# The bias of an output projection, moved from a TensorE product and a ScalarE copy to one VectorE pass, in a four-engine attention pipeline

## The reference

```python
h = jnp.maximum(_layernorm(x, axis=-1), 0.0)
x = x + _L0_gnn_ref(h, adj, adj, L0_gnn_b)          # (128, 128, 256) + a number per row
h = jnp.maximum(_layernorm(x, axis=-1), 0.0)
...
qkv = (x @ w_qkv).reshape(b, n, 3, H, hd).transpose(2, 0, 3, 1, 4)      # 8 heads of 32
attn = jnp.einsum('bhnd,bhmd->bhnm', q, k) * scale
attn = jnp.where(attn_mask[None, None] == 0, -jnp.inf, attn)
attn = jax.nn.softmax(attn, axis=-1)
o = jnp.einsum('bhnm,bhmd->bhnd', attn, v).transpose(0, 2, 1, 3).reshape(b, n, d)
o = o @ w_proj + b_proj
mu = jnp.mean(o, axis=-1, keepdims=True)
var = jnp.mean(jnp.square(o - mu), axis=-1, keepdims=True)
ln = (o - mu) * jax.lax.rsqrt(var + LN_EPS) * ln_gamma + ln_beta
return o + ln
```

## Time and profile before

| | us |
|---|---|
| median of 3 runs | 870.18 |
| lowest, highest | 869.18, 874.16 |
| profiled execution, its own time | 871.38 |
| its span | 869.7 |
| PE busy | 765.6 (88%) |
| DVE busy | 613.9 (71%) |
| ACT busy | 500.7 (58%) |
| POOL busy | 424.7 (49%) |

### The profile page before, as it was taken

How to read it: one execution, slowest core, us unless ns; L and a number is a source line. 1 busy time by engine, 2 the same in 40 slices (tenths; PEclk the granted TensorE clock), 3 DMA queues, 4 the chain that set the end, 5 groups by cost and what they waited for, 6 DMA issues and landing times.

```text
span 869.7 us, 31246 instructions
## 1 busy us (share of the span) xinstructions
PE 765.6 (88%) x11241; PEld 518.0 (60%) x11241; DVE 613.9 (71%) x1552; ACT 500.7 (58%) x1192; POOL 424.7 (49%) x853
## 2 busy tenths in 40 slices
...
GB/s 190 64 155 145 124 159 138 173 145 128 168 163 137 155 151 159 104 171 163 141 159 169 128 137 160 156 150 172 157 137 146 162 148 166 129 133 120 51 46 25
DMA packets 167271, 121.34 MB, mean 140 GB/s; under 512 B 83696, under 2 KB 166384, under 8 KB 166640
## 3 DMA queue, kind: packets, MB, share of 16 engines
...
q0 software_dynamic: 16896, 16.78, 14.2%
...
## 4 chain that ended last, share of the span: by engine, by line
PE 72%; issue 8%; ACT 6%; DVE 5%; SPq 3%; POOL 3%; DMA 2%; ACTq 1%; DVEq 0%; POOLq 0%
PE a_ps L319 17%; PE a_ps L332 9%; PE sum_ps L446 9%; PE pv_ps L416 8%; PE sc_ps L368 7%; PE sum_ps L419 6%; PE sc_ps L396 5%; PE sc_ps L344 4%; PE a_ps L304 4%; SPq L273 3%; DVE smax L674 2%; ACT h_sb L516 2%; PE pv_ps L431 2%; PE sum_ps L443 2%; ACT o_sb L590 1%
## 5 line engine op out<-in xcount | busy, mean ns | idle before, releaser
L674 DVE TENSOR_REDUCE smax<-sc_ps 128x4 f32<-128x512 f32 x256 | 164.8, 685 | 53.7 <-PE sc_ps L368 51.6
L571 ACT ACTIVATE p_sb<-sc_ps 128x512 f32<-128x512 f32 x256 | 145.8, 599 | 45.9 <-PE sum_ps L419 36.9
L666 DVE TENSOR_TENSOR pairs<-a_ps,pairs 128x512 f16<-128x512 f32 x128 | 87.5, 684 | 110.7 <-ACT pairs L561 110.2
L841 POOL TENSOR_TENSOR h_parts<-h_sb,h_parts 128x256 f16<-128x256 f32 x128 | 84.2, 669 | 141.5 <-ACT h_parts L524 141.2
L319 PE MATMUL a_ps<-hT,w_hi 128*128 128x512 f16 x512 | 141.0, 400 | 13.7 <-DMA hT<-h_parts 13.7
L847 POOL TENSOR_TENSOR oT_lo<-oT,oT_hi 128x256 f16<-128x256 f32 x128 | 85.6, 669 | 119.5 <-ACT oT_hi L584 119.3
L561 ACT ACTIVATE pairs<-a_ps 128x512 f16<-128x512 f32 x128 | 75.9, 594 | 97.8 <-PE a_ps L319 85.0
L416 PE MATMUL pv_ps<-p_sb,v_sb 128*32 128x128 f32 x2048 | 107.6, 279 | 20.1 <-DVE crow L680 10.3
L878 POOL DMA_DIRECT2D out<-y_sb x32 | 43.6, 1363 | 141.4 <-DVE y_sb L730 141.4
L419 PE MATMUL sum_ps<-p_sb,sel_sum 128*32 128x128 f32 x2048 | 105.3, 274 | 0.0
L368 PE MATMUL sc_ps<-stack 96*128 96x128 f16 x1024 | 86.0, 226 | 6.7 <-DMA stack<-pairs 6.5
...
## 6 DMA issues: line engine op xcount, KB each, us to landing
...
stack<-crow SPq DMA_DIRECT2D x64, 8.0 KB, 3.9
...
hT<-h_parts ACTq DMA_TRANSPOSE x32, 6.0
```

Source lines behind the costliest of these rows:

```text
L571: nc.scalar.activation(p_sb[:, u % P_SLOTS], sc_ps[u % SC_SLOTS][:], ACT.Exp, scale=SCALE).then_inc(p_ready, 1)
L666: nc.vector.tensor_tensor(pairs[:, 1 - c % 2, c // 2, c % 2], a_ps[c % 2][:], pairs[:, c % 2, c // 2, c % 2], ALU.subtract).then_inc(qklo_ ...
L674: nc.vector.tensor_reduce(smax[:, HC * j:HC * (j + 1), b], sc_ps[u % SC_SLOTS][:], AX.X, ALU.max).then_inc(smax_ready, 1)
L841: nc.gpsimd.tensor_tensor(h_parts[:, par, 1, b], h_sb[:, b], h_parts[:, par, 0, b], ALU.subtract).then_inc(hlo_ready, 1)
```

## The change

The bias is no longer a product. `project_o` has six products instead of seven, and `take_o` goes from ACT to DVE: one `scalar_tensor_tensor` reads `o_ps`, scales it and adds the bias, which all partitions hold (`bproj_sb`). The constants that split the bias go away. The orders of PE, ACT, DVE and POOL are changed.

```diff
-ACT_CONST = 5
-DVE_CONST = 14 + 2
+ACT_CONST = 4
+DVE_CONST = 7
...
-                nc.tensor.matmul(o_ps, bias_ones[:], bp_rows[:], start=True, stop=False)
                 for k, (o, w) in enumerate(((oT_hi, wp_hi), (oT_hi, wp_lo), (oT_lo, wp_hi))):
                     for j in range(DC):
-                        mm = nc.tensor.matmul(o_ps, o[:, b, j], w[:, j], start=False, stop=(k == 2 and j == DC - 1))
+                        mm = nc.tensor.matmul(o_ps, o[:, b, j], w[:, j], start=(k == 0 and j == 0), stop=(k == 2 and j == DC - 1))
                 mm.then_inc(o_psum, 1)
...
-            ORDER = ("K0 S0 S1 R0 S2 Q0 S3 R1 Q1 N0 E0 R2 O0 E1 E2 E3 L0 O1 R3 K1 S4 S5 O2 S6 S7 L1 O3 N1 M0 E4 E5 E6 "
-                     "P0 P1 Q2 P2 P3 Q3 P4 P5 E7 V0 P6 P7 V1").split()
+            ORDER = ("K0 S0 S1 R0 S2 S3 Q0 R1 Q1 R2 N0 E0 E1 E2 O0 L0 E3 R3 O1 K1 S4 S5 S6 L1 O2 S7 O3 N1 M0 E4 P0 P1 "
+                     "Q2 E5 P2 P3 Q3 E6 E7 P4 P5 V0 P6 P7 V1").split()
...
-                nc.scalar.activation(bp_parts[:, 0], bproj_sb[:], ACT.Copy).then_inc(act_const, 1)
...
-            def take_o(g, b):
-                act.wait_ge(o_psum, G * g + b + 1)
-                if b == 0:
-                    wait(act, tw_ready, G * g)
-                nc.scalar.activation(o_sb[:, b], o_ps, ACT.Copy, scale=1.0 / (OS * WS)).then_inc(o_ready, 1)
...
+            def take_o(g, b):
+
+                dve.wait_ge(o_psum, G * g + b + 1)
+                if b == 0:
+                    wait(dve, tw_ready, G * g)
+                nc.vector.scalar_tensor_tensor(o_sb[:, b], o_ps, 1.0 / (OS * WS), bproj_sb[:], ALU.mult,
+                                               ALU.add).then_inc(o_ready, 1)
...
-            ORDER = ("I0 I1 I2 S0 O0 S1 S2 S3 O1 Q0 O2 X0 Q1 L0 B0 O3 S4 B1 S5 S6 S7 B2 B3 M0 X1 G0 L1 Q2 F0 Q3 F1 F2 "
-                     "F3").split()
+            ORDER = ("I0 I1 I2 S0 O0 S1 S2 O1 S3 Q0 O2 X0 Q1 A0 O3 L0 A1 B0 S4 S5 B1 A2 S6 S7 A3 B2 M0 B3 G0 L1 F0 F1 "
+                     "Q2 F2 F3 Q3 X1").split()
...
-            ORDER = ("C0 Q0 R0 R1 C1 Q1 E0 C2 O0 E1 E2 E3 H0 O1 X0 C3 R2 O2 H1 H2 O3 R3 M0 H3 E4 A0 T0 Q2 A1 E5 Q3 E6 "
-                     "E7 A2 V0 A3 V1 L0").split()
...
+            ORDER = ("R0 C0 R1 H0 Q0 H1 Q1 C1 C2 E0 E1 E2 E3 X0 R2 H2 R3 C3 H3 M0 E4 A0 L0 T0 A1 Q2 E5 Q3 A2 E6 E7 A3 "
+                     "V0 V1").split()
```

More of the change, by code:

```diff
@@ L77, in build @@
         bproj_sb = sb("bproj_sb", [P, D])
-        bproj_r1 = sb("bproj_r1", [P, D])
-        bproj_r2 = sb("bproj_r2", [P, D])
         bias0_sb = sb("bias0_sb", [P, 1])
@@ L88, in build @@
         mask_k = sb("mask_k", [P, ROW_TILES, N], BF16)
-        bp_parts = sb("bp_parts", [P, 3, D], F16)
-        bp_rows = sb("bp_rows", [P, D], F16)
-        bias_ones = sb("bias_ones", [P, P], F16)
         identf = sb("identf", [P, P])
@@ L615, in step @@
                         take_pv(t - 2, i)
-                    elif kind == "O" and d:
-                        take_o(t - 3, i)
                     elif kind == "C" and d:
@@ L744, in step @@
                         scale_o(t - 3, i)
+                    elif kind == "A" and d:
+                        take_o(t - 3, i)
                     elif kind == "B" and d:
@@ L776, in later_constants @@
             def later_constants():
-                nc.vector.memset(bias_ones[:], OS * WS).then_inc(dve_const, 1)
-                nc.vector.memset(bp_rows[:], 0.0).then_inc(dve_const, 1)
                 nc.vector.tensor_scalar(mask_n[:, 0], adj_sb[:], 0.0, MASKED, ALU.is_equal, ALU.mult).then_inc(dve_const, 1)
@@ L788, in later_constants @@
                                         ALU.add).then_inc(dve_const, 1)
-                dve.wait_ge(act_const, 5)
-                nc.vector.tensor_tensor(bproj_r1[:], bproj_sb[:], bp_parts[:, 0], ALU.subtract).then_inc(dve_const, 1)
-                dve.wait_ge(dve_const, DVE_CONST - 6)
-                nc.vector.tensor_copy(bp_parts[:, 1], bproj_r1[:]).then_inc(dve_const, 1)
-                dve.wait_ge(dve_const, DVE_CONST - 5)
-                nc.vector.tensor_tensor(bproj_r2[:], bproj_r1[:], bp_parts[:, 1], ALU.subtract).then_inc(dve_const, 1)
-                dve.wait_ge(dve_const, DVE_CONST - 4)
-                nc.vector.tensor_copy(bp_parts[:, 2], bproj_r2[:]).then_inc(dve_const, 1)
-                dve.wait_ge(dve_const, DVE_CONST - 3)
-                for i in range(3):
-                    nc.vector.tensor_copy(bp_rows[HD * i:HD * i + 1], bp_parts[HD * i:HD * i + 1, i]).then_inc(dve_const, 1)
             stats_x(0, 0)
@@ L878, in store @@
                 nc.gpsimd.dma_start(og[g], y_sb[:], accum_op=ALU.add).then_inc(stored, 16)
-            ORDER = ("C0 C1 C2 H0 C3 H1 H2 H3 N0 W0 W1 W2 W3 K0 D0 X0").split()
+            ORDER = ("C0 C1 H0 C2 C3 H1 H2 H3 N0 W0 W1 K0 W2 W3 D0 X0").split()
             def step(t, k, a, sc, e, d, prep, norm, load):
```

## The result

The changed kernel took 908.49 us as a median of 4 runs (902.86 to 909.23), the kernel before 871.6 us as a median of 4 (869.18 to 874.16). The ratio is 1.0409, with a 95% interval of 1.0355 to 1.0463: 36.9 us slower, where 44 were forecast. The profiled execution took 908.0, its span is 906.2 us. Now and then a run is over 1.5% longer than the fastest of its kernel; the ratios leave such runs out (in o2_ahead two of four), the medians keep them.

What follows compares the result with a forecast made beforehand. PE was taken as the bound, with DVE tied at N1. Steps of +1.65 us (0.6 + 0.44 + 0.6) in 20, +0.95 in 9, and 2 at the start gave +44 us: 914, range 888 to 932.

Steps and rivals of the forecast that it cites:

- Term 1: DVE's queue ahead of N1: added takes make the eighth row maximum late, P0 +0.6 us per step.
- Term 2: PE behind P0: E5 and E6 now stand there, where PE is the bound, +0.44 us per step.
- the start: Before the full steps: Q0 and Q1 on ACT wait for POOL's shift, +2 us, bounds 0 and +3.
- the end: Last three steps: 0.1 less on PE and 0.04 more on the take per element cancel, 0.
- term 3: Second half of the stack: Q3 on DVE behind F delays its DMAs, S4 +0.6 us, between 0 and 1.2.
- the stalls: About 9 steps that begin with a stall: stack lateness counts nothing there, +0.95 us each, 9 us.
- The walk through the queues: Following PE's and DVE's new orders up to P0: eighth maximum ends at 12.3, N1 starts at 12.36.
- The rival of 948: New PE waits lower the clock in 20 steps, 1.7 us each; chance 0.10 shared with a slow take.

Runs made afterwards that it cites:

- o2_ahead: Changed kernel with O2 ahead of S6 on PE and B1 behind the last take on DVE; 894.02 us, ratio 1.0175 to the kernel before.
- stats_in_gap: Changed kernel with the statistics of x on DVE moved behind L1, where DVE waits for POOL; 908.76 us, ratio 1.0433 to the kernel before.
- e5_e6_ahead: Changed kernel with E5 and E6 ahead of P0 on PE, as before; 930.93 us, ratio 1.0634 to the kernel before.
- e5_e6_x_later: The e5_e6_ahead kernel with the load of x moved behind C3 on ACT; 906.73 us, ratio 1.0419 to the kernel before.
- all_undone: Changed kernel with O2, B1, E5, E6, Q2, Q3, X1, POOL's shift and the load of x moved, other orders kept; 878.04 us, ratio 1.0043.
- orders_alone: Kernel before, bias product on PE and takes on ACT kept, with the changed kernel's orders; 917.4 us, ratio 1.0489.

## Why the prediction came out as it did

The sign and the mechanism held: slower, by a longer step, through the chain at N1, the products behind P0 and the stack. The forecast of 914 was 5.5 us too high, and +44 stands against +36.9. The number came out nearer than its terms, and that is luck: terms 1 and 2 gave 2.6 us more than predicted, the start 3.3 and the end 2.1 more, term 3 some 7 less and the stalls 7 less.

- **The take**: 0.42 us and 54 us were predicted, 0.419 and 53.7 measured. L703 was the right row.
- **Term 1**: N1 at 12.36 and P0 at 14.2 were predicted, 12.59 and 14.39 measured in the step shown; less the late stack (0.18) that is 12.41. The size is right; the argument by a sum is not. The prediction summed all of DVE's work from the first maximum to the eighth (10.9 us against 9.9) and called the idle time used up. stats_in_gap took 1.3 us out of that stretch, and N1 came 0.24 earlier at most. PE hands over S4, and the chain to N1 starts anew there: 0.56 of the 0.68 come from A2 between the fifth and the eighth maximum, and from O2 that comes late for it. A sum over 11 us hid that. The walk through the queues in the prediction did have A2's wait (0.23 predicted, 0.21 seen), which is why its number came out.
- **The waits of PE**: 0.3, 0.5, 0.5 and 0.9 were predicted at O1, O3, N1 and P0; the brackets show 0.17, 0.38, 0.29 and 0.82, at the right places. At O1 the bracket names the low part on POOL, which ended at 465.04, 0.01 behind the take A0, so both held it.
- **Term 2**: P0 to K0 went from 9.81 to 10.26 where 10.25 was predicted. Undoing it gave that back in e5_e6_ahead but not in time, since it also made the stack due earlier: a cost that is at the same time cover for another one.
- **Terms 1 and 2 together** are 1.04 per step predicted, 1.09 measured (24.46 against 23.37): 31.6 us in 29 steps, against 29 in the sum, which had 0.95 in the steps with a stall.
- **Term 3** was mis-sized: +0.6 in 20 steps, 12 us, was predicted. Q3 ends 7.90 behind P0 (predicted 8.0), SP's twelve take 9.68 (9.8), and the stack is used 2.06 after the last issue (2.1). So the ready time of 9.1 should have been 8.9, and in the first step shown S4 came at 8.73, due at 8.55. The lateness is the small difference of two large sums, 0.2 in the mean of the 29 steps and not 0.6 in 20 of them, and PE's waits for the stack outside the start are 11.1 - 3.71 - 2.88 = 4.5 us. What the prediction did not see at all is that the change also moved the load of x on ACT to just behind the last stack DMA: SP in the changed kernel has `455.46 9.49`, so its last issue starts at 464.35, and the load is issued at 465.13, 0.78 behind it, where it was 1.92 in the step of the earlier trace rows. Some tenths more and the landing doubles, as e5_e6_ahead and, in three steps, o2_ahead show (S4 there waits 2.79 us with the load issued at 480.13 and SP's last at 480.05). The rival of 948 had idle time that lowers the granted clock. Such idle time exists (3.01 us in e5_e6_ahead), but P0's 0.82 is not enough of it: in the changed kernel's step shown above (457.70 to 482.30) the granted clock is 1.00.
- **The start**: +2 was predicted, the first `RECIPROCAL` is 5.3 later. Q2 of the first step comes 2.3 us later (40.47 against 38.20), as argued. The rest lies in steps 1 and 2: K0 of step 1 is 2.15 later, of step 2 3.18, of step 3 5.33. PE waits for the stack in both, 3.71 and 2.88 us, where it waited 3.58 and 2.55 before, so the waits themselves are only 0.46 of it:

```profile
58.67 1.46 PE L363 MATMUL sc_ps<-stack 96*128 96x128 f16 x12 [3.71 <-DMA stack<-pairs]
...
81.12 1.42 PE L363 MATMUL sc_ps<-stack 96*128 96x128 f16 x12 [2.88 <-DMA stack<-pairs]
```

  In step 1, M0 now waits 0.79 for the row maximum. In step 2, S4 to N1 is 0.93 longer, and P0 to K0 takes 12.42 us at a granted clock of 0.82, before 11.09 at 0.88: 0.45 of that is term 2. The rest goes with the clock, which fell after the wait in both kernels (0.51 in the 5.77 us up to P0, before 0.61 in 5.28) and came back later here. The wait in step 2 is 1.26 in e5_e6_x_later and gone in all_undone, where P0 to K0 is 9.8 and the first `RECIPROCAL` comes at 93.78 and 92.09.
- **The stalls**: the steps that begin a round cost some 7 us less in excess of the normal step than before, which the prediction did not have. The wait in them, `issue` at K0, is the same (15.2 and 15.5 us). PE's waits for `pv_sb` fall from 9.8 us to under 1. That fits, since E5 now stands between P1 and P2, but orders_alone has as few such waits (1.1 us) and no such gain, so this stays open.

The 0.39 us in the queue that the prediction estimated by the Trainium skill (Perfetto Trace Analysis, Optimizing Scalar/DVE Operations) is not what the trace shows: A1 to B1 and A3 to B2 start 0.34 and 0.33 us apart.
